# An expert stage with its gates in two SBUF copies, and no product that spreads them

## The reference

```
z = einsum('nd,sdr->nsr', xf, P)
scores = einsum('nsr,smr->nsm', z, C)
topv, topi = top_k(scores, 4);  w = softmax(topv)
h = gelu(einsum('nsr,nskrh->nskh', z, W1[topi]) + b1[topi])
yl = einsum('nskh,nskhr->nskr', h, W2[topi]) + b2[topi]
comb = einsum('nskr,nsk->nsr', yl, w)
out = gelu(comb @ G1 + g1b) @ G2 + g2b
```

## Time and profile before

| | us |
|---|---|
| three runs | 1804.47, 1804.54, 1810.88 (median 1804.54) |
| the profiled execution, span | 1811.7 |
| TensorE busy | 1622.6 (90%) |
| VectorE busy | 1351.4 (75%) |
| ScalarE busy | 1095.4 (60%) |
| GpSimd busy | 718.0 (40%) |
| SP's and other DMA queues | 102.38 MB, engines 21.1% busy for the main queue |

### The profile page before, as it was taken

How to read it: one execution, slowest core, us unless ns; L and a number is a source line. 1 busy time by engine, 2 the same in 40 slices (tenths; PEclk the granted TensorE clock), 3 DMA queues, 4 the chain that set the end, 5 groups by cost and what they waited for, 6 DMA issues and landing times.

```text
span 1811.7 us, 31074 instructions
## 1 busy us (share of the span) xinstructions
PE 1622.6 (90%) x8824; PEld 674.4 (37%) x8824; DVE 1351.4 (75%) x2824; ACT 1095.4 (60%) x2122; POOL 718.0 (40%) x656
## 2 busy tenths in 40 slices
PE   5974888888888888874999999999999999999997
PEld 3631665555666665661122222222222212222221
DVE  4471488878888878875878877878878878878874
ACT  0131244545444445522888888888888888888884
POOL 4460366656666666663222222222222222222221
PEclk9755899989999999985899999999999999999998
DMA  7337012112112221114211121212212121121200
GB/s 225 99 92 85 22 42 80 57 55 65 55 55 58 72 77 56 58 50 112 51 26 43 38 51 25 66 32 48 49 25 56 30 56 40 39 51 25 66 24 9
DMA packets 120652, 102.38 MB, mean 57 GB/s; under 512 B 16951, under 2 KB 117743, under 8 KB 120175
## 3 DMA queue, kind: packets, MB, share of 16 engines
q1 hardware_dynamic: 117097, 94.99, 21.1%
q0 software_dynamic: 2112, 3.79, 0.8%
q10 hardware_dynamic: 1376, 2.88, 0.5%
HBM read 58.74 MB, written 39.62 MB: 54 GB/s over the span
## 4 chain that ended last, share of the span: by engine, by line
PE 73%; DVE 13%; issue 5%; POOL 3%; ACT 3%; DMA 2%; SPq 0%; DVEq 0%; POOLq 0%; ACTq 0%
PE pair L1546 22%; PE bank L1573 20%; PE bank L1561 6%; PE bank L1478 4%; PE pair L1447 4%; DVE arena L1118 3%; PE pair L1458 3%; PE pair L1417 2%; PE pair L1416 2%; DVE arena L1098 2%; PE bank L1366 2%; DVE arena L1107 2%; DVE arena L1201 1%; PE bank L1589 1%; PE bank L1440 1%
## 5 line engine op out<-in xcount | busy, mean ns | idle before, releaser
L1326 DVE TENSOR_TENSOR arena<-arena,bank 128x1984 f32<-128x1984 f32 x336 | 734.1, 2218 | 176.2 <-ACT arena L936 162.1
L936 ACT ACTIVATE arena<-pair 128x992 f32<-128x992 f32 x768 | 739.0, 998 | 156.7 <-PE pair L1546 156.7
L740 POOL TENSOR_TENSOR arena<-arena 128x992 f32<-128x992 f32 x96 | 219.1, 2304 | 698.0 <-PE bank L1573 685.0
L1546 PE MATMUL pair<-arena,w_stack 99*128 99x496 bf16 x1536 | 459.5, 382 | 13.6 <-ACT arena L936 13.6
L1573 PE MATMUL bank<-arena,w_pad 128*32 128x496 f32 x3072 | 399.0, 592 | 1.2 <-DVE arena L1326 1.2
L1546 PEld LDWEIGHTS pair<-arena,w_stack 99*128 99x128 bf16 x1536 | 88.1, 97 | 412.0 <-ACT arena L936 311.5
L1561 PE MATMUL bank<-arena,sel 48*128 48x496 bf16 x384 | 147.0, 383 | 0.6 <-ACT arena L838 0.6
L1573 PEld LDWEIGHTS bank<-arena,w_pad 128*32 128x32 f32 x3072 | 60.8, 108 | 160.4 <-issue 158.3
L1458 PE MATMUL pair<-arena 128*128 128x94 f32 x768 | 110.2, 306 | 2.6 <-DVE arena L1165 2.4
L1478 PE MATMUL bank<-arena 128*124 128x192 f32 x576 | 106.9, 337 | 3.7 <-POOL arena L675 3.7
L1458 PEld LDWEIGHTS pair<-arena 128*128 128x128 f32 x768 | 106.6, 222 | 3.3 <-DVE arena L1165 2.6
(11 more groups left out here) (141 smaller groups left out, 1929.0 us busy)
## 6 DMA issues: line engine op xcount, KB each, us to landing
gate_parts<-arena SPq DMA_DIRECT2D x48, 372.0 KB, 6.7
arena<-gate_parts SPq DMA_DIRECT2D x576, 31.0 KB, 1.8
arena<-h_scratch SPq DMA_DIRECT2D x32, 279.0 KB
arena<-z_parts SPq DMA_DIRECT2D x144, 62.0 KB, 2.2
h_scratch<-arena SPq DMA_DIRECT2D x16, 279.0 KB
z_parts<-arena SPq DMA_DIRECT2D x48, 93.0 KB, 1.7
arena<-h_scratch SPq DMA_DIRECT2D x12, 372.0 KB
out_h<-arena SPq DMA_DIRECT2D x12, 372.0 KB
```

The lines of the kernel that those rows point to most:

```text
L740: p_.tensor_tensor(gated[:, block % 2, j, pair], hid[:, quad % 4, pair], gcopy.unsqueeze(1).to_broadcast([128, 2, TN]), ALU.mult).then_inc ...
L936: a_.activation(hid[:, quad % 4, 2 * (pair % 2):2 * (pair % 2) + 2], (pair0, pair1)[pair % 2][:, :, 0:TN], ACT.Gelu_apprx_tanh).then_inc(s ...
L1326: v_.tensor_tensor(gated[:, block % 2, j], hid[:, quad % 4], gate_banks[quad % 2][:, 0:TN].unsqueeze(1).to_broadcast([128, KH, TN]), ALU.m ...
L1546: mm = t_.matmul((pair0, pair1)[pair % 2][:, a, 0:TN], w1s[:, x:x + 128], zst[:, o, j], start=True, stop=True)
```

## The change

The expert stage works in duos: a duo is a row of 64 experts by 2 units, two of them, so 2 x 496 columns, half of what a quad was; a tile has 64.

- With 64 experts in a row, the two units of an expert lie 64 rows apart, and each gate is needed only twice. SP loads the fp32 gates of one half of the groups twice, to rows 0 to 63 and 64 to 127 of `gst` (two transfers a half tile). The product `spread`, `sel`, `gate_banks` and ScalarE's copy of the gates go.
- In PSUM there are three pairs for the hidden products, not two (`RING`). Every gelu writes SBUF: three buffers of a duo for VectorE (`hidv`), two for GpSimd (`hid`).
- VectorE multiplies 42 of 64 duos, GpSimd 22 (those with d % 11 in 2, 5, 8, 10, without the 32nd). Both read `hidv` or `hid` and the gates in SBUF.
- TensorE makes both hidden pairs of a quad, then the decode. `decode` waits for half a block at a time.
- Stage 2 keeps the gates in fp32: one copy by ScalarE (`gates_copy`) in place of part 1, rest, part 2 and part 3; `bias` makes 4 fp32 products in place of 24 bf16 ones; one gate store in place of three.
- Stage 1: b2 is placed in fp32, without parts. w1, b1 and w2 are reordered: ScalarE and VectorE read w1 in four strided pieces, b1 comes in 8 loads, and w2 in 32 loads that SP issues between the text stores, behind a wait for the eighth image product.

The diff, cut to its core:

```
+DUOS = 2 * QUADS
+POOL_DUOS = [d for d in range(DUOS) if d % 11 in (2, 5, 8, 10) and d != 32]
+DVE_LIST = [d for d in range(DUOS) if d not in POOL_DUOS]
+RING = [d % 3 for d in range(DUOS - 4)] + [0, 1, 0, 2]
...
-        gst = c3(128, [8, 2, TN], BF16)
+        gst = c3(128, [2, PAIRS, TN])
-        hid = c3(128, [4, KH, TN])
+        hid = c3(128, [2, 2, TN])
+        hidv = c3(128, [3, 2, TN])
...
+            sp.wait_ge(s_ips, 8)
+            w2_from = t["w2"].rearrange("(m g a) (s e x) -> a e g m s x", m=16, a=2, s=S, e=EB)
+            for a in range(2):
+                for e in range(EB):
+                    for g in range(EB):
+                        rows = slice(64 * a + 16 * e, 64 * a + 16 * e + 16)
+                        sp.dma_start(w2f[rows, g], w2_from[a, e, g]).then_inc(s_w2f, 16)
...
+            def load_gates(tile, o):
+                for h in range(2):
+                    sp.dma_start(gst[64 * h:64 * h + 64, o],
+                                 gq_r[o, :, :, bass.ds(tile * TN, TN)]).then_inc(s_gl[o], 16)
...
+            def refill(tile, o):
+                wait_apart(sp, (s_hp1, DUOS * (tile - 1) + DUOS // 2 * (o + 1)))
+                load_codes(tile, o)
+                last = DUOS // 2 * (o + 1) - 1
+                wait_apart(sp, (s_gat, dve_gated(tile - 1, last)), (s_pg, pool_gated(tile - 1, last)))
+                load_gates(tile, o)
...
-            def gate_part3(u, s):
-                pool.wait_ge(s_g2, SUB * u + s + 1)
-                p_.tensor_tensor(gh[:, 2, :, ST * s:ST * s + ST], grr[:, s],
-                                 gh[:, 1, :, ST * s:ST * s + ST], ALU.subtract).then_inc(s_g3, 1)
...
+            def gate_duo(tile, duo):
+                quad, a = divmod(duo, 2)
                 block, j = divmod(quad, PAIRS)
+                if duo == first_pool[block // EB]:
+                    pool.wait_ge(s_gl[block // EB], 32 * (tile + 1))
+                if first_of_half_block(duo, POOL_DUOS):
+                    wait(pool, s_code, QUADS * tile + PAIRS * (block - 2) + 2 * a + 2)
+                pool.wait_ge(s_hid, DUOS * tile + duo + 1)
+                p_.tensor_tensor(gated[:, block % 2, j, 2 * a:2 * a + 2], hid[:, POOL_DUOS.index(duo) % 2],
+                                 gst[:, block // EB, j].unsqueeze(1).to_broadcast([128, 2, TN]),
+                                 ALU.mult).then_inc(s_pg, 1)
...
+            def gelu(tile, duo):
+                act.wait_ge(s_hp1, DUOS * tile + duo + 1)
+                product = ring[RING[duo]][:, :, 0:TN]
+                if duo in POOL_DUOS:
+                    wait(act, s_pg, pool_gated(tile, duo) - 2)
+                    a_.activation(hid[:, POOL_DUOS.index(duo) % 2], product, ACT.Gelu_apprx_tanh).then_inc(s_hid, 1)
+                else:
+                    wait(act, s_gat, dve_gated(tile, duo) - 3)
+                    a_.activation(hidv[:, DVE_LIST.index(duo) % 3], product, ACT.Gelu_apprx_tanh).then_inc(s_hid, 1)
...
-                v_.tensor_tensor(gated[:, block % 2, j], hid[:, quad % 4],
-                                 gate_banks[quad % 2][:, 0:TN].unsqueeze(1).to_broadcast([128, KH, TN]),
+                v_.tensor_tensor(gated[:, block % 2, j, 2 * a:2 * a + 2], hidv[:, DVE_LIST.index(duo) % 3],
+                                 gst[:, block // EB, j].unsqueeze(1).to_broadcast([128, 2, TN]),
                                  ALU.mult).then_inc(s_gat, 1)
...
-                for i in range(6):
-                    for j in range(PAIRS):
-                        mm = t_.matmul(pair1[32 * j:32 * j + 32, 0, 0:UT], b2p[:, j, WP[i]], gh[:, ZP[i], j],
-                                       start=(i == 0), stop=(i == 5), skip_group_check=True)
+                for j in range(PAIRS):
+                    mm = t_.matmul(pair1[32 * j:32 * j + 32, 0, 0:UT], b2p[:, j], gh[:, j], start=True, stop=True)
...
             def decode(tile, block, k):
-                if k == 0:
-                    pe.wait_ge(s_gat, dve_gated(tile, PAIRS * block + PAIRS - 1))
-                    wait(pe, s_pg, 2 * pool_quads(tile, PAIRS * block + PAIRS - 1))
+                if k % 2 == 0:
+                    needed = 2 * (PAIRS * block + PAIRS - 1) + k // 2
+                    pe.wait_ge(s_gat, dve_gated(tile, needed))
+                    pe.wait_ge(s_pg, pool_gated(tile, needed))
...
                 for quad in range(QUADS):
-                    spread_next(quad)
                     hidden_ahead(quad, AHEAD)
+                    hidden_ahead(quad, AHEAD + 1)
                     decode_next(quad)
-                    hidden_ahead(quad, AHEAD + 1)
```

More of the change, by code:

```diff
@@ L80, in wait, with dve_gated, pool_gated, same_buffer_before @@
     eng.wait_ge(sem, value)
[L83 to L90, removed]
+def dve_gated(tile, duo):
+    return DVE_DUOS * tile + sum(d not in POOL_DUOS for d in range(duo + 1))
+def pool_gated(tile, duo):
+    return len(POOL_DUOS) * tile + sum(d <= duo for d in POOL_DUOS)
+def same_buffer_before(tile, duo):
+    for d in range(duo - 1, -1, -1):
+        if RING[d] == RING[duo]:
+            return tile, d
+    return tile - 1, max(d for d in range(DUOS) if RING[d] == RING[duo])
+def first_of_half_block(duo, mine):
+    return not any(d in mine for d in range(duo - duo % 8 + duo % 2, duo, 2))
 def build(nc, t):
@@ L557, in _ @@
                     load_h1(tile)
-                    for q in range(4):
-                        refill(tile + 1, q)
+                    for o in range(2):
+                        refill(tile + 1, o)
             load_bias(TILES - 1)
@@ L746, in add_bias @@
                 p_.tensor_tensor(code, comb, bias_t, ALU.add).then_inc(s_cb, 1)
+            first_pool = [min(d for d in POOL_DUOS if d >= DUOS // 2 * o) for o in range(2)]
             def pool_tile(tile, first):
-                for quad in POOL_QUADS:
-                    gate_quad(tile, quad)
-                    if quad == POOL_QUADS[0] and not first:
+                for duo in POOL_DUOS:
+                    gate_duo(tile, duo)
+                    if duo == BIAS_AFTER and not first:
                         add_bias(tile - 1)
@@ L953, in tile_act @@
             def tile_act(tile, first):
-                for pair in range(2 * QUADS):
-                    gelu(tile, pair)
-                    if pair % 2 == 1 and pair // 2 in POOL_QUADS:
-                        copy_gates(tile, pair // 2)
+                for duo in range(DUOS):
+                    gelu(tile, duo)
                     if not first:
-                        if pair == 9:
+                        if duo == 9:
                             copy_code(tile - 1)
-                        if pair == 2 * OUT1_AT + 5:
+                        if duo == 2 * OUT1_AT + 5:
                             gelu_out(tile - 1)
@@ L1283, in pass_dve @@
                     logits_max(a)
-                if has(g):
-                    rest(g, 0)
                 if has(a):
@@ L1342, in tile_dve @@
             def tile_dve(tile, par, first):
[L1343 to L1345 removed]
+                for duo in range(DUOS):
+                    if duo not in POOL_DUOS:
+                        gate_duo(tile, duo)
                     if not first:
                         for half in range(2):
[L1348 removed]
+                            if duo == 2 * OUT2_AT[half] + 3:
                                 add_out(tile - 1, half, 1 - par)
@@ L1626, in tile_pe @@
                                 out2(tile - 1, half)
-            spread(0, 0)
-            for pair in range(AHEAD):
-                hidden(0, pair)
+            for duo in range(AHEAD):
+                hidden(0, duo)
             tile_pe(0, True, False)
```

280 lines of the change are left out of this document (92 added, 188 removed).

## The result

The changed kernel takes 1993.16 us (median of 4 runs, 1984.49 to 1993.80) against 1806.76 (4 runs, 1804.47 to 1810.88): a ratio of 1.102 (95% interval 1.099 to 1.106), 10% slower. 2002.5 was predicted. The profiled execution spans 1992.1 us, 180.4 more than the 1811.7 of before.

The account below looks back on a forecast made before the run. TensorE bounds the expert stage at 77.67 us a tile; afterwards VectorE and GpSimd, taking turns on SBUF, at 95. Expert stage +208, stage 2 -14, stage 1 +4 make +198: median 2002.5 us, range 1949 to 2094.

Parts of the forecast that it names:

- the turns: Expert stage: VectorE with two SBUF operands and a reading GpSimd instruction take turns; tile 95 us instead of 77.67.
- The sum: Expert stage: VectorE's and GpSimd's turns in a tile without gaps, 93.7 us; 95 taken with the output additions.
- The 208 us: Expert stage: 17.3 us more per tile, times twelve, +208 us (bounds +159 and +299).
- upper sum: Expert stage: tile if nothing of VectorE and GpSimd overlaps and the additions count, 102.6 us; time some 2095.
- the -14: Stage 2: total saving from removed operations, -14 us (bounds -4 and -20).
- Its first term: Stage 2: third normalisation no longer held by GpSimd's removed subtraction, 0.74 us in each of 14 passes, 10.4 in all.
- The tail's term, -3.5: End of stage 2: shorter bare chain from last gate copy to bias copy, 5.2 us before, saving 3.5.
- +4: Stage 1: w2 loads on SP delay a text store and VectorE's addition 6 us, 2 made up; bounds 0 and +12.
- +198: Whole kernel: +208 expert stage, -14 stage 2, +4 stage 1; profiled span about 2010 us, median 2002.5.
- A: Rival, expert stage: VectorE and GpSimd overlap, TensorE stays the bound at 67.8 us a tile; 1675 us; chance 0.08.
- B: Rival, expert stage: TensorE's clock falls and makes it the bound, below a mean of 0.68; 2140 to 2350 us; chance 0.06.
- C: Rival, expert stage: ScalarE held by full buffers, gaps over 0.2 us between turns; 2095 us and more; chance 0.03.

Follow-up runs that it names:

- e3: Changed kernel, 42/22 split kept, but VectorE's gelus stay in their PSUM pair and VectorE multiplies from there; 1839.43 us, ratio 1.018 to the kernel before.
- e1: Changed kernel with all 64 duos multiplied by VectorE, none by GpSimd, and four gelu buffers; 1785.32 us, ratio 0.989 to the kernel before.
- e2: Changed kernel with 10 of 64 duos on GpSimd instead of 22, 54 on VectorE; 1834.27 and 1849.3 us, ratio 1.020 to the kernel before.
- e4: Changed kernel plus one unused GpSimd subtraction per pass of stage 2; 2027.22 (profiled) and 2005.53 us, ratio 1.117 to the kernel before.

## Why the prediction was right, and where its sizes were off

**What bounds the kernel, and the turns: right.** The sum was 93.7 us a tile, 95 was taken, and the eleven measured distances are 94.0 to 95.1 us but for the first, of 92.4. In one tile of 95.0, one of VectorE and GpSimd or both are at a multiplication or the bias addition for 93.85 us. The terms hold one by one: 1.174 and 2.293 us undisturbed (predicted 1.18 and 2.30), 1.102 from start to start of two of VectorE's in a row (1.10), and 3.3 at the worst for either. The overlaps came from rows of stage 2 whose instructions were half as large or smaller; e3 shows that it is the kind of operands and not the stage. The 208 us were 203.6 in the span. The alternation that the prediction read off one collision held too: of 206 GpSimd instructions between 950 and 1800 us 200 had their turn after the one of VectorE that was running.

**The length of a turn.** The two floors add up to 3.47 us, and the longest instruction of either took 3.30 and 3.33: 0.14 to 0.17 us at a change of hands is free, near the 0.13 to 0.15 that the prediction had read. By the Trainium skill (SBUF — State Buffer, section "Who interferes with whom") an instruction holds the shared pair of ports from its start to its end, and the tile would be 102.6 us by the prediction's upper sum, an estimate. With 94.7 measured, the trace agrees with the turn and not with its full length.

**Stage 2: the mechanism right, the size half.** The step that was mis-sized is the -14, where -28.5 were measured. Its first term, 0.74 us in each pass, measures 0.76. What it left out is TensorE's clock, which it treated as given: 10.1 us of the 20.0 over 13 passes are stretches at the lower level that became shorter. The windows of the earlier trace rows showed a clock of 0.87 in this stage, and one pass in the trace of before took 45.4 us; a look at the lengths of all passes would have raised the question. The tail's term, -3.5, held from the last gate copy to the bias copy: 2.16 us where it had been 5.20, -3.0. Behind it 3.3 more went, from that copy to the first multiplication (9.18 to 5.87). All of it is in two places on the chain. GpSimd's `memset` at the head of the expert stage (lines 730 and 733), on which ScalarE's first gelu waits, starts when the last bias store has landed. That took 4.29 us from its issue before, behind three gate stores, and 1.97 after, behind one:

```profile
851.87 4.29 DMA bias_codes<-arena
```

```profile
831.97 1.97 DMA bias_codes<-arena
```

From that `memset` on it was 4.17 us to the first multiplication and is 3.18, since a duo needs one gelu and a quad needed two. The prediction had not looked past the bias copy. The rest, -1.5 us ahead of the 13 passes and -0.7 in the tail, no run explains.

**Stage 1: the place right, the size near.** The wait was named at its line and its time and put at 6 us, of which 2 would be made up; it is 8.94, and 6.6 of it are left from the sixth addition on (71.9 to 78.5 us). That addition came 1.3 us earlier in this execution, which gives the +5.3. That +4 and +5.3 are so near is partly luck: the end of stage 1 wanders by 13 us between executions.

**The error.** On the span: -4.4 for the turns, -14.5 for stage 2, +1.3 for stage 1, together 17.6 less than +198. The median missed by only 9.3, since the profiled execution of before was the longest of its runs, as the prediction took into account, and that of after lies within 1.1 us of its median.

**The rivals.** A (no turns, 1675): refuted by the lengths of lines 1293 and 744 and by e1 and e2. B (the clock makes TensorE the bound): the granted clock of the tile above is 0.88, far over 0.68, and TensorE stands idle for 225.3 us before its hidden products. It does fall and rise all through the stage, from 1.00 to 0.88 in the mean, which costs nothing while VectorE and GpSimd are the bound. C (gaps): VectorE's idle time before its multiplications is 29.0 us in the whole stage, 2.4 a tile.

## What to carry to other kernels

Before an elementwise operation is moved from a PSUM operand to two SBUF operands, find out who else works with two SBUF operands at that time: VectorE and GpSimd then add up instead of overlapping, and here a second engine that needs 2.3 us for what the first does in 1.2 was worse than none. Two tensors in SBUF are not the only such case: the normalisation of stage 2 reads one tensor from SBUF, with a factor and an offset per row, and goes from 0.37 to 1.11 us beside GpSimd. Here the saving on TensorE (9.9 us a tile) was real and turned into -5% only when GpSimd was taken out of the stage altogether, down to its one short addition. In a trace the sign is a floor and a ceiling: if an instruction's longest time is its shortest plus the other engine's, they take turns, and busy shares of the two can't be added as if they were independent.

## What was not expected of the hardware

**GpSimd may get no turn.** Against VectorE's multiplications in an unbroken row GpSimd's addition waited 11 times of 11 through 14 of them (16.3 us for 1.23) and ended only when VectorE ran dry. In e2 104 of 113 GpSimd instructions between 950 and 1800 us had their turn after the one VectorE instruction that was running, one after two, and 8 after five (up to 6.76 us). How long VectorE's next gelu had been ready doesn't separate the cases: 0.5 to 3.1 us where GpSimd was passed over, and from not at all to 5.4 us where it got its turn. What does is open, and no run was made on it. A GpSimd instruction on which something waits is therefore not bounded by one VectorE instruction.

**The clock follows small changes.** A subtraction of 1 us on GpSimd goes with passes of 45.3 us instead of 39.7 at the most, four times in 13 in the profiled execution of e4, by stretches at the lower level.
